# Feed-forward stage: rotating x in slices of 128 columns, with the 4-point levels on VectorE

## The chip, the cores and the metric

The kernel runs on one core of one Trainium2 chip. The metric is the device time of one execution in microseconds (us), lower is better. In the tables and rows PE is TensorE (PEld its weight load), DVE is VectorE, ACT is ScalarE, POOL is GpSimd and SP is SyncE.

## The reference

The input x is 128 batches of 32 tokens of 512 channels, 4096 rows in all. Three blocks are added to it in turn: cross attention over a context, a delta-rule attention with an MLP, and a feed-forward block. Only the last one is touched:

```python
def fwht(x):   # normalized Walsh-Hadamard transform of the last axis, n a power of 2
    h = 1
    while h < n:
        a, b = halves of each 2h columns
        x = stack([a + b, a - b]); h *= 2
    return x / sqrt(n)

def act_quant(x):  # per row
    scale = 127 / clip(max(abs(x)), EPS)
    return clip(round(x * scale), -128, 127) / scale

def h_bitlinear(x, w): return act_quant(fwht(x)) @ ternary(w).T

h = layernorm(x)                       # 512 wide
y = silu(h_bitlinear(h, w_gate)) * h_bitlinear(h, w_up)   # 2048 wide
x = x + h_bitlinear(y, w_down)         # 512 wide
```

So each row of h is rotated by a 512-point transform, and each row of y by a 2048-point one. Each is then rounded with a step that comes from the largest magnitude of its own row.

## The kernel before

Four phases follow one another: attention, delta rule, MLP, feed-forward (`ffn_phase`, line 1901). The MLP phase writes the normalised rows `xn`. The feed-forward phase works through 32 tiles of 128 rows (NT = 32). Five engine programs run side by side and hold a software pipeline: step k of each (`body(k, do)`) works on several tiles at once. Tile k is in its "main" part, tile k+1 in "one" (rotate and round x), tile k+2 in "two" (load and transpose x), tile k-1 in "mid" (butterflies of y on GpSimd), tile k-2 in "end" (round the rotated y, down projection) and tile k-3 in "sum". Steps -2 to 34 run, and an engine executes its instructions in the order written. Semaphores join the engines. PSUM banks are passed round in rings: `take` waits until a bank is full, `open` until it is free, `used` until it has been freed.

What each engine does in one step, in this order:

- TensorE: gates and ups of tile k (line 2008, 8 groups of four 512-column matmuls, through 4 banks), `rotate_x` of tile k+1 (line 1990), transposes of x of tile k+2 (1982), transposes of y (2017), of the first half of rounded z of tile k-2 (2034), `rotate_y` (2025) of the first half, transposes of the second half of z, `rotate_y` of the second half, transposes of rounded x (1999), down projection of tile k-2 (2042).
- ScalarE: waits for the factor of z (`q2`), then four times silu of a gate (2093) and scaling of a quarter of z (2096); the high part of xT (2101), four copies of yT (2105), scaling of the rotated x into `xs` (2109), then twice a copy of ziT (2114) and of zo (2118), and last the copy of xiT (2121).
- VectorE: largest magnitude of z (2217) with small operations for its factor, output sum (2211), four products y (2191) with the clipping of the first half of z (2186) in front of the last of them, the low part of xT (2179), the clipping of the second half of z (2186), then `round_x`: largest magnitude of the rotated x (2159) and five small operations (2161 to 2167). After it come `clip_x` (2174), which waits for `xs`, and `first_level`, four 512-column sums and differences (2202, 2203) in two pairs, each of which waits for ScalarE's zo.
- GpSimd: once `first_level` of tile k-1 is complete, six 1024-column sums and differences (2141 and 2142 in turn: zb, za, z), all with both operands in SBUF.

`rotate_x` takes the transposed x as a high and a low f16 part (`xT[:, 0]` and `xT[:, 1]`, n = 0, 1) and, for each of four 128-channel blocks c, multiplies it by 512 columns of the Hadamard matrix, all eight matmuls accumulating in one bank. That bank ("had", ring RX) is read by line 2159 on VectorE and by line 2109 on ScalarE, which frees it.

Of the kernel before, what the change touches and what calls it, by code (L numbers as in the profile page):

```python
# [7 lines left out]
P = 128  # L8
D = 512
DC = D // P  # L10
# [16 lines left out]
ALU = mybir.AluOpType  # L27
ACT = mybir.ActivationFunctionType
AXX = mybir.AxisListType.X


class Store:
# [6 lines left out]
    def sb(self, name, shape, dt=F32):  # L39
        return self.ctx.enter_context(self.nc.sbuf_tensor(self.tag + name, shape, dt))  # L40
# [4 lines left out]
    def sem(self, name):  # L45
        self.taken.append(self.ctx.enter_context(self.nc.semaphore(self.tag + name)))
        return self.taken[-1]
# [1853 lines left out]
def ffn_phase(nc, x2, xn, shared, out):  # L1901
# [5 lines left out]
    with ExitStack() as stack:  # L1907
# [8 lines left out]
        amax, step_, inv1, fac1 = (sb(n, [P, 1]) for n in ("amax", "step", "inv1", "fac1"))  # L1916
        gsc = sb("gsc", [P, 2])
        xs = sb("xs", [P, D])
        xq = sb("xq", [P, D], BF16)
        ident16 = sb("ident16", [P, P], BF16)  # L1920
        xiT = sb("xiT", [P, DC, P], BF16)
# [16 lines left out]
        y_ready, zo_ready, first, bf, am2, q2, zs_ready, clip2 = (  # L1938
            sem(n) for n in ("y_ready", "zo_ready", "first", "bf", "am2", "q2", "zs_ready", "clip2"))
        dsc_ready, summed = sem("dsc"), sem("summed")  # L1940

        def steps(eng, body):

# [30 lines left out]
        @block.tensor  # L1974
        def _(pe):
            pe.wait_ge(set_ready, 2)

            def transpose_x(i, r):
                p, full = RX.open(pe, r, "xT")
                pe.wait_ge(xn_ready, 16 * (i + 1))  # L1980
                for c in range(DC):
                    mm = pe.transpose(p[:, c * P:(c + 1) * P], xn_t[:, c * P:(c + 1) * P], ident[:])  # L1982
                mm.then_inc(full, 1)

            def rotate_x(i, r):
                RX.used(pe, r - 1, "xT")
                p, full = RX.open(pe, r, "had")
                for c in range(DC):
                    for n in range(2):
                        mm = pe.matmul(p[:], xT[:, n, c * P:(c + 1) * P], had[:, c, :],  # L1990
                                       start=(c + n == 0), stop=(c + n == DC))
                mm.then_inc(full, 1)

            def transpose_xi(i, r):
                p, full = RX.open(pe, r, "xiT")
                p = p[:].bitcast(BF16)
                pe.wait_ge(clip1, i + 1)
                for c in range(DC):
                    mm = pe.transpose(p[:, c * P:(c + 1) * P], xq[:, c * P:(c + 1) * P], ident16[:])
                mm.then_inc(full, 1)  # L2000

            def gates(i, r):
                RX.used(pe, r - 1, "xiT")
                for j in range(NB):
                    for n, w in (("g", w_g), ("u", w_u)):
                        p, full = RM.open(pe, i, f"{n}{j}")
                        for c in range(DC):
                            mm = pe.matmul(p[:], xiT[:, c, :], w[:, c, j * 512:(j + 1) * 512],  # L2008
                                           start=(c == 0), stop=(c == DC - 1))
                        mm.then_inc(full, 1)  # L2010

            def transpose_y(i):
                for j in range(NB):
                    p, full = RM.open(pe, i, f"yT{j}")
                    pe.wait_ge(y_ready, i * NB + j + 1)
                    for c in range(4 * j, 4 * j + 4):
                        mm = pe.transpose(p[:, c % 4 * P:(c % 4 + 1) * P], y[:, c * P:(c + 1) * P], ident[:])
                    mm.then_inc(full, 1)

            def rotate_y(i, js):  # L2020
                for j in js:
                    p, full = RM.open(pe, i, f"z{j}")
                    RM.used(pe, i, f"yT{j}")
                    for c in range(4):
                        mm = pe.matmul(p[:, c * P:(c + 1) * P], yT[:, 4 * j + c, :], had1, start=True, stop=True)  # L2025
                    mm.then_inc(full, 1)

            def transpose_zi(i, h):
                p, full = RQ.open(pe, i, f"zi{h}")
                p = p[:].bitcast(BF16)  # L2030
                pe.wait_ge(clip2, 2 * i + h + 1)
                for j in range(WC // 2):
                    c = WC // 2 * h + j
                    mm = pe.transpose(p[:, j * P:(j + 1) * P], zq[:, c * P:(c + 1) * P], ident16[:])
                mm.then_inc(full, 1)

            def down(i):
                p, full = RQ.open(pe, i, "down")
                for c in range(WC):
                    if c % (WC // 2) == 0:  # L2040
                        RQ.used(pe, i, f"zi{c // (WC // 2)}")
                    mm = pe.matmul(p[:], ziT[:, c, :], w_d[:, c, :], start=(c == 0), stop=(c == WC - 1))
                mm.then_inc(full, 1)
                RQ.skip(pe, i, "pad")

            def body(k, do):
                r = k + 2
                if do["main"]:
                    gates(k, r)
                if do["one"]:  # L2050
                    rotate_x(k + 1, r)
                else:
                    RX.skip(pe, r, "had")
                if do["two"]:
                    transpose_x(k + 2, r)
                else:
                    RX.skip(pe, r, "xT")
                if do["main"]:
                    transpose_y(k)
                if do["end"]:  # L2060
                    transpose_zi(k - 2, 0)
                if do["main"]:
                    rotate_y(k, (0, 1))
                if do["end"]:
                    transpose_zi(k - 2, 1)
                if do["main"]:
                    rotate_y(k, (2, 3))
                if do["one"]:
                    transpose_xi(k + 1, r)
                else:  # L2070
                    RX.skip(pe, r, "xiT")
                RX.skip(pe, r, "pad")
                if do["end"]:
                    down(k - 2)

            steps(pe, body)

        @block.scalar
        def _(act):
# [3 lines left out]
            def body(k, do):  # L2083
# [5 lines left out]
                for j in range(NB):  # L2089
                    if do["main"]:  # L2090
                        p, free = RM.take(act, k, f"g{j}")
                        act.wait_ge(y_ready, k * NB + max(j - 1, 0))
                        A.activation(sg[:, j % 2, :], p[:], ACT.Silu, scale=gsc[:, 0:1]).then_inc(free, 1)  # L2093
                    if do["end"]:
                        cols = slice(j * 512, (j + 1) * 512)
                        A.activation(zs[:, cols], z[:, cols], ACT.Identity, scale=fac2[:, 0:1], bias=offset[:, 0:1])\  # L2096
                            .then_inc(zs_ready, 1)
                if do["two"]:
                    p, _ = RX.take(act, r, "xT")
                    RX.take(act, r, "had")  # L2100
                    A.activation(xT[:, 0, :], p[:], ACT.Copy, scale=HS).then_inc(xT_hi, 1)  # L2101
# [3 lines left out]
                        A.copy(yT[:, 4 * j:4 * j + 4, :].rearrange("p c n -> p (c n)"), p[:]).then_inc(free, 1)  # L2105
                if do["one"]:
                    act.wait_ge(q1, 3 * (k + 2))
                    p, free = RX.take(act, r, "had")
                    A.activation(xs[:], p[:], ACT.Identity, scale=fac1[:, 0:1], bias=offset[:, 0:1]).then_inc(free, 1)
                for h in range(2):  # L2110
                    if do["end"]:
                        p, free = RQ.take(act, i, f"zi{h}")
# [36 lines left out]
        def _(dve):  # L2149
# [5 lines left out]

            def round_x(i, r):

                p, _ = RX.take(dve, r, "had")
                V.tensor_reduce(amax[:], p[:], AXX, ALU.max, apply_absolute_value=True).then_inc(am, 1)  # L2159
                dve.wait_ge(am, 3 * i + 1)  # L2160
                V.tensor_scalar(step_[:], amax[:], D ** -0.5 / HS, QEPS, ALU.mult, ALU.max).then_inc(am, 1)
                dve.wait_ge(am, 3 * i + 2)
                V.reciprocal(inv1[:], step_[:]).then_inc(am, 1)
                dve.wait_ge(am, 3 * i + 3)
                V.tensor_scalar(fac1[:], inv1[:], QMAX, D ** -0.5 / HS, ALU.mult, ALU.mult).then_inc(q1, 1)
                for n in range(2):
                    V.tensor_scalar(gsc[:, n:n + 1], step_[:], wscale[:, n:n + 1], 1.0 / QMAX, ALU.mult, ALU.mult)\
                        .then_inc(q1, 1)

            def clip_x(i, r):  # L2170
                RX.used(dve, r, "had")
                if not (isinstance(i, int) and i == 0):
                    RX.take(dve, r - 1, "xiT")
                V.tensor_scalar(xq[:], xs[:], MAGIC + QMAX, MAGIC, ALU.min, ALU.subtract).then_inc(clip1, 1)
# [164 lines left out]
```

## Time and profile before

| what | value |
|---|---|
| median of 3 runs | 3093.07 us (3091.05 to 3095.14) |
| profiled execution, own time | 3089.57 us |
| its span | 3087.7 us |
| PE busy over the span | 2757.9 us (89%) |
| DVE busy | 1990.8 us (64%) |
| ACT busy | 1436.7 us (47%) |
| POOL busy | 1009.8 us (33%) |

The span runs from the first to the last instruction that the profiler saw. The feed-forward phase begins about 2424 us into it and lasts to the end. Ends of matmuls are modelled, so a busy TensorE is not one at its peak; starts of successive groups are the better clock.

### The profile page before, as it was taken

What the parts mean: (1) busy time and instruction counts of PE and PEld (TensorE: products, weight loads), DVE (VectorE), ACT (ScalarE), POOL (GpSimd) and SP (SyncE); (2) the same over time, 40 slices, a digit from 0 to 9 for tenths busy, and PEclk for the clock granted to TensorE, in tenths of its full rate; (3) what the DMA queues carried; (4) which work ended last, traced back from release to release, by engine and by line L of the source; (5) the groups of instructions that cost most, each with busy time, mean ns of one, the idle gap of its engine ahead of it and who ended that gap; (6) DMA issues with size and microseconds to landing.
All of it is one profiled execution on the core that took longest, in us unless ns stands there. A gap on an engine that the chain in (4) does not pass through costs nothing. (4 is left out here: it accounts for less than half of the span.)

```text
span 3087.7 us, 66709 instructions
## 1 busy us (share of the span) xinstructions
PE 2757.9 (89%) x26968; PEld 1466.9 (48%) x26968; DVE 1990.8 (64%) x2991; ACT 1436.7 (47%) x2378; POOL 1009.8 (33%) x713
## 2 busy tenths in 40 slices
PE   6999999686888888888855999999999699999997
PEld 3444444252544444444433444444444366666664
DVE  3444444459989898898993544545543377777775
ACT  2222222375767758667632432222222256666664
POOL 0000000107538346274481000000000177777776
PEclk9999999888998989889866999999999899999998
DMA  6999888500000000000040032332120111111110
GB/s 241 336 334 332 312 284 310 176 15 1 2 29 2 29 13 19 29 2 29 16 155 21 22 111 94 101 104 96 66 71 28 66 38 41 41 41 41 41 37 31
DMA packets 126284, 290.20 MB, mean 94 GB/s; under 512 B 30480, under 2 KB 35216, under 8 KB 121968
## 3 DMA queue, kind: packets, MB, share of 16 engines
q1 hardware_dynamic: 122608, 261.85, 24.4%
q10 hardware_dynamic: 3456, 25.17, 2.4%
q8 instruction: 169, 2.77, 0.4%
q14 instruction: 51, 0.42, 0.0%
HBM read 244.96 MB, written 42.01 MB: 93 GB/s over the span
## 5 line engine op out<-in xcount | busy, mean ns | idle before, releaser
L2141 POOL TENSOR_TENSOR d_zb<-d_za 128x1024 f32<-128x1024 f32 x32 | 75.3, 2354 | 955.7 <-DVE d_za L2203 955.7
L899 PE MATMUL b_e<-b_hT,s_region 128*128 128x512 f16 x1152 | 283.3, 392 | 49.1 <-DVE s_region L1327 36.5
L1629 PE MATMUL c_r<-c_hT,c_g_pair 128*128 128x512 f16 x1056 | 244.4, 382 | 1.6 <-DVE c_hT L1805 1.6
L2008 PE MATMUL d_m<-s_region,d_xiT 128*128 128x512 bf16 x1024 | 238.4, 384 | 5.1 <-ACT d_xiT L2121 1.6
L1629 PE MATMUL c_r<-c_hT,c_u_pair 128*128 128x512 f16 x1056 | 242.3, 379 | 0.0
L1629 PE MATMUL c_d<-c_d_pair,c_aT 128*128 128x512 f16 x1056 | 242.1, 379 | 0.0
L1819 DVE SCALAR_TENSOR_TENSOR c_av<-c_r,c_sg 128x512 f32<-128x512 f32 x88 | 60.8, 691 | 271.7 <-PE c_r L1629 211.2
L1327 DVE SCALAR_TENSOR_TENSOR s_region<-b_e,b_cw,s_region 128x496 f32<-128x496 f32 (+2 forms) x288 | 203.0, 716 | 18.3 <-ACT s_region L1117 9.9
L851 POOL TENSOR_TENSOR b_tmp<-b_L,s_hn 128x496 f32<-128x496 f32 (+30 forms) x124 | 122.5, 988 | 260.9 <-ACT b_L L1100 251.5
L851 POOL TENSOR_TENSOR b_tmp<-b_L,b_U 128x496 f32<-128x496 f32 (+30 forms) x124 | 130.8, 1055 | 223.8 <-ACT b_L L1100 214.4
L899 PEld LDWEIGHTS b_e<-b_hT,s_region 128*128 128x128 f16 x1152 | 104.0, 100 | 190.0 <-DVE s_region L1327 44.2
L1729 ACT ACTIVATE c_sg<-c_r 128x512 f32<-128x512 f32 x88 | 52.5, 596 | 255.2 <-PE c_r L1629 255.1
L1629 PEld LDWEIGHTS c_r<-c_hT,c_g_pair 128*128 128x128 f16 x1056 | 103.8, 99 | 127.3 <-issue 2.8
L2008 PEld LDWEIGHTS d_m<-s_region,d_xiT 128*128 128x128 bf16 x1024 | 96.3, 99 | 141.6 <-DVEq L2194 16.3
L1629 PEld LDWEIGHTS c_r<-c_hT,c_u_pair 128*128 128x128 f16 x1056 | 103.3, 98 | 124.6
L268 POOL COPY a_kx<-a_kl 128x64 f32<-128x64 f32 x8 | 2.5, 313 | 485.3 <-PE a_ps L314 469.8
L1733 ACT CAST c_aT<-c_av 128x512 f16<-128x512 f32 x88 | 54.3, 617 | 229.5 <-DVE c_av L1819 229.5
L1629 PEld LDWEIGHTS c_d<-c_d_pair,c_aT 128*128 128x128 f16 x1056 | 103.3, 98 | 121.5 <-DVE c_aT L1824 0.2
L2093 ACT ACTIVATE d_sg<-d_m,d_gsc 128x512 f32<-128x512 f32 x128 | 87.2, 681 | 150.0 <-DVE d_fac L2223 140.6
L1377 DVE TENSOR_TENSOR b_U<-b_U,b_tmp 128x1488 f32<-128x1488 f32 (+30 forms) x124 | 145.4, 1172 | 4.3
L985 PE MATMUL b_r<-b_wo,b_xg 128*128 128x512 f32 x256 | 146.1, 688 | 0.0
L853 POOL TENSOR_TENSOR b_U<-b_U,b_tmp 128x496 f32<-128x496 f32 (+30 forms) x124 | 141.8, 1143 | 9.7
(255 smaller groups left out, 6029.7 us busy)
## 6 DMA issues: line engine op xcount, KB each, us to landing
a_cT<-in_ctxT SPq DMA_DIRECT2D x128, 512.0 KB, 9.7
a_cn<-in_ctx SPq DMA_DIRECT2D x128, 512.0 KB, 9.1
a_x_ln<-in_x SPq DMA_DIRECT2D x8, 1024.0 KB, 16.1
a_cw<-in_ctx SPq DMA_DIRECT2D x128, 64.0 KB, 9.5
a_x_res<-in_x SPq DMA_DIRECT2D x32, 256.0 KB, 11.4
x<-a_x_out SPq DMA_DIRECT2D x32, 256.0 KB, 11.3
b_xg<-x SPq DMA_DIRECT2D x8, 1024.0 KB, 5.5
om<-b_hT SPq DMA_DIRECT2D x32, 256.0 KB, 2.0
```

Source lines behind the costliest of these rows:

```text
L851: nc.gpsimd.tensor_tensor(tmp[:, QV, s + 1:S, :], lo, us, ALU.mult).then_inc(pool_prod, 1)
L853: nc.gpsimd.tensor_tensor(U[:, QV, s + 1:S, :], U[:, QV, s + 1:S, :], tmp[:, QV, s + 1:S, :], ALU.subtract).then_inc(pool_sub, 1)
L899: mm = pe.matmul(p[:], w_qkv[:, a, i, n, c * P:(c + 1) * P], hp[:, b, n, :], start=(n + a + b == 0), stop=(n == DC - 1 and a == 1))
L985: mm = pe.matmul(p[:], oT[:, c, t * P:(t + 1) * P], w_o[:, c, :], start=(c == 0), stop=(c == DC - 1))
L1327: ins = V.scalar_tensor_tensor(acc[:, :, j:S], src[:, :, 0:S - j], cw[:, i, c, TAPS - 1 - j:TAPS - j], acc[:, :, j:S], ALU.mult, ALU.add)
L1377: V.tensor_tensor(U[:, 0:QV, s + 1:S, :], U[:, 0:QV, s + 1:S, :], tmp[:, 0:QV, s + 1:S, :], ALU.subtract).then_inc(sub, 1)
L1629: mm = pe.matmul(out, x, y, start=start and i == 0, stop=stop and i == 2)
L1733: A.copy(aT[:, f % 2, 0, :], av[:]).then_inc(a_hi, 1)
L1819: V.scalar_tensor_tensor(av[:], p[:], AS / (WS * HS), sg[:, f % 2, :], ALU.mult, ALU.mult)\
L2008: mm = pe.matmul(p[:], xiT[:, c, :], w[:, c, j * 512:(j + 1) * 512], start=(c == 0), stop=(c == DC - 1))
L2093: A.activation(sg[:, j % 2, :], p[:], ACT.Silu, scale=gsc[:, 0:1]).then_inc(free, 1)
L2141: nc.gpsimd.tensor_tensor(o[:, :, 0, :], a[:, :, 0, :], a[:, :, 1, :], ALU.add).then_inc(bf, 1)
```

## The change

`rotate_x` multiplies each of the four 128-channel blocks by the 128-point Hadamard matrix alone and leaves the result in that block's own 128 columns of the bank. The eight matmuls keep their weights, and their columns go from 512 to 128. What is missing, a 4-point transform across the four slices, is done in two levels after it. ScalarE copies the odd slices (1 and 3) from PSUM to SBUF (`xo`, 256 columns). VectorE forms even + odd and even - odd from PSUM and `xo` into `xa`, two operations of 256 columns, and then frees the bank. From the two halves of `xa` it forms sum and difference into `xr`, again two operations of 256 columns, with both operands in SBUF. The largest magnitude is taken of `xr`, and ScalarE scales `xr` instead of the bank.

```diff
+        xo, xa, xr = sb("xo", [P, 2, P]), sb("xa", [P, 2, 2, P]), sb("xr", [P, 2, 2, P])
+        xo_ready, xl = sem("xo_ready"), sem("xl")
 rotate_x (TensorE):
-                        mm = pe.matmul(p[:], xT[:, n, c * P:(c + 1) * P], had[:, c, :],
-                                       start=(c + n == 0), stop=(c + n == DC))
+                        mm = pe.matmul(p[:, c * P:(c + 1) * P], xT[:, n, c * P:(c + 1) * P], had[:, 0, 0:P],
+                                       start=(n == 0), stop=(n == 1))
 body (ScalarE), between the scalings of z and the high part of xT:
+                if do["one"]:
+                    p, _ = RX.take(act, r, "had")
+                    A.copy(xo[:], p[:].rearrange("p (m two h) -> p m two h", two=2, h=P)[:, :, 1, :])\
+                        .then_inc(xo_ready, 1)
 body (ScalarE), scaling of x:
                 if do["one"]:
                     act.wait_ge(q1, 3 * (k + 2))
-                    p, free = RX.take(act, r, "had")
-                    A.activation(xs[:], p[:], ACT.Identity, scale=fac1[:, 0:1], bias=offset[:, 0:1]).then_inc(free, 1)
+                    A.activation(xs[:], xr[:].rearrange("p a b h -> p (a b h)"), ACT.Identity, scale=fac1[:, 0:1],
+                                 bias=offset[:, 0:1]).then_inc(xs_ready, 1)
 round_x (VectorE):
-                p, _ = RX.take(dve, r, "had")
-                V.tensor_reduce(amax[:], p[:], AXX, ALU.max, apply_absolute_value=True).then_inc(am, 1)
+                p, free = RX.take(dve, r, "had")
+                dve.wait_ge(xo_ready, i + 1)
+                even = p[:].rearrange("p (m two h) -> p m two h", two=2, h=P)[:, :, 0, :]
+                V.tensor_tensor(xa[:, :, 0, :], even, xo[:], ALU.add).then_inc(xl, 1)
+                V.tensor_tensor(xa[:, :, 1, :], even, xo[:], ALU.subtract).then_inc(xl, 1)
+                dve.wait_ge(xl, 4 * i + 2)
+                dve.sem_inc(free, 1)
+                V.tensor_tensor(xr[:, 0], xa[:, 0], xa[:, 1], ALU.add).then_inc(xl, 1)
+                V.tensor_tensor(xr[:, 1], xa[:, 0], xa[:, 1], ALU.subtract).then_inc(xl, 1)
+                dve.wait_ge(xl, 4 * i + 4)
+                V.tensor_reduce(amax[:], xr[:].rearrange("p a b h -> p (a b h)"), AXX, ALU.max, apply_absolute_value=True).then_inc(am, 1)
 clip_x (VectorE):
-                RX.used(dve, r, "had")
+                dve.wait_ge(xs_ready, i + 1)
```

## Rows read from the trace of the kernel before

**Rows 1.** Busy time by stretch: us, each engine's busy us (instructions), PEclk, DMA, GB/s
```profile
2500.00:2600.00 100.00, 99.45 (x657) 63.18 (x656) 76.41 (x122) 60.11 (x98) 75.79 (x32) 1.00 0.12 39
2900.00:3000.00 100.00, 99.61 (x655) 62.74 (x653) 76.01 (x122) 59.10 (x95) 75.57 (x32) 1.00 0.12 39
```
**Rows 2.** Timeline, one step, TensorE: start us, us, engine line op, tiles, [idle before]
```profile
2528.41 3.62 PE L2042 MATMUL d_q<-s_region,d_ziT 128*128 128x512 bf16 x16
2531.86 7.43 PE L2008 MATMUL d_m<-s_region,d_xiT 128*128 128x512 bf16 x32
2539.13 1.89 PE L1990 MATMUL d_x<-s_region,d_xT 128*128 128x512 f16 x8
2540.86 0.60 PE L1982 MATMUL d_x<-s_ident,d_xn 128*128 128x128 f32 x4
2543.04 0.61 PE L2034 MATMUL d_q<-d_ident,d_zq 128*128 128x128 bf16 x8
2543.49 2.00 PE L2025 MATMUL d_m<-s_region,d_yT 128*128 128x128 f32 x16
```
**Rows 3.** Timeline, the same step, VectorE and ScalarE, to the next first level
```profile
2530.34 0.68 DVE L2203 TENSOR_TENSOR d_za<-d_m,d_zo 128x512 f32<-128x512 f32 x1
2535.66 0.75 DVE L2191 SCALAR_TENSOR_TENSOR d_y<-d_m,d_gsc,d_sg 128x512 f32<-128x512 f32 x1
2539.02 2.05 DVE L2186 TENSOR_SCALAR d_zq<-d_zs 128x1024 bf16<-128x1024 f32 x1 [0.32 <-DVE d_y L2191]
2539.08 0.81 ACT L2096 ACTIVATE d_zs<-d_z,d_offset,d_fac 128x512 f32<-128x512 f32 x1
2540.99 0.74 DVE L2191 SCALAR_TENSOR_TENSOR d_y<-d_m,d_gsc,d_sg 128x512 f32<-128x512 f32 x1
2542.12 0.69 DVE L2179 SCALAR_TENSOR_TENSOR d_xT<-d_x,d_xT 128x512 f16<-128x512 f32 x1 [0.40 <-ACT d_xT L2101]
2542.73 1.12 DVE L2186 TENSOR_SCALAR d_zq<-d_zs 128x1024 bf16<-128x1024 f32 x1
2543.78 0.68 DVE L2159 TENSOR_REDUCE d_amax<-d_x 128x1 f32<-128x512 f32 x1
2545.31 0.78 ACT L2109 ACTIVATE d_xs<-d_x,d_offset,d_fac 128x512 f32<-128x512 f32 x1 [1.27 <-DVE d_gsc L2167]
2546.22 0.43 DVE L2174 TENSOR_SCALAR d_xq<-d_xs 128x512 bf16<-128x512 f32 x1 [0.95 <-ACT d_xs L2109]
2546.88 0.60 ACT L2118 COPY d_zo<-d_m 128x512 f32<-128x512 f32 x1
2547.67 0.69 DVE L2202 TENSOR_TENSOR d_za<-d_m,d_zo 128x512 f32<-128x512 f32 x1 [1.02 <-ACT d_zo L2118]
2549.79 0.68 DVE L2203 TENSOR_TENSOR d_za<-d_m,d_zo 128x512 f32<-128x512 f32 x1
```
**Rows 4.** Timeline, the same step, GpSimd: first and last three of its six
```profile
2531.10 2.36 POOL L2141 TENSOR_TENSOR d_zb<-d_za 128x1024 f32<-128x1024 f32 x1 [4.48 <-DVE d_za L2203]
2538.16 2.36 POOL L2142 TENSOR_TENSOR d_za<-d_zb 128x1024 f32<-128x1024 f32 x1
2540.75 2.55 POOL L2141 TENSOR_TENSOR d_z<-d_za 128x1024 f32<-128x1024 f32 x1 [0.24 <-POOL d_za L2142]
2543.26 2.80 POOL L2142 TENSOR_TENSOR d_z<-d_za 128x1024 f32<-128x1024 f32 x1
```
**Rows 5.** Timeline, delta phase: VectorE and GpSimd, both with two SBUF operands
```profile
1098.32 0.77 POOL L853 TENSOR_TENSOR b_U<-b_U,b_tmp 128x272 f32<-128x272 f32 x1
1099.17 1.73 POOL L851 TENSOR_TENSOR b_tmp<-b_L,b_U 128x256 f32<-128x256 f32 x1
1100.42 1.74 DVE L1377 TENSOR_TENSOR b_U<-b_U,b_tmp 128x1200 f32<-128x1200 f32 x1
```
**Rows 6.** Timeline, delta phase, GpSimd idle: VectorE sum and ScalarE copies near 256 columns
```profile
1406.91 0.35 ACT L1167 COPY s_xt<-b_e 128x256 f32<-128x256 f32 x1
1407.16 0.60 ACT L1168 COPY s_region<-b_e 128x256 f32<-128x256 f32 x1
...
1428.92 0.41 DVE L1377 TENSOR_TENSOR b_U<-b_U,b_tmp 128x240 f32<-128x240 f32 x1
```
**Rows 7.** Busy time by stretch at the phase's start (columns as in rows 1)
```profile
2468.00:2472.00 4.00, 2.18 (x19) 1.61 (x18) 3.79 (x4) 1.24 (x3) 1.76 (x1) 0.99 0.00 0
2472.00:2476.00 4.00, 4.00 (x13) 1.47 (x11) 3.62 (x7) 0.22 (x1) 3.11 (x2) 0.59 0.01 2
```

## The prediction

> **What bounds the kernel now.** The change lies wholly in the feed-forward phase, so I read that alone. The busy times by stretch come first: TensorE shows 99.5 busy in 100 us and VectorE 76 [rows 1], which invites the verdict that TensorE is the bound and that thinner matmuls help. The timeline of one step must confirm it. Steps repeat: `first_level` ends at 2530.34 + 0.68 = 2531.02 and next at 2549.79 + 0.68 = 2550.47 [rows 3], so a step takes 19.43 to 19.45 us. I call the first of these moments F, and give the rest as a distance from it.
>
> TensorE's order is full or nearly so. By starts, 16 down matmuls take 2531.86 - 2528.41 = 3.45 us, 216 ns each [rows 2]. The 32 gate matmuls take 2539.13 - 2531.86 = 7.27 us where 32 x 216 ns = 6.91, so TensorE stands about 0.36 us in each step, waiting in the middle of the gates for silu and y. It is not the sole bound, therefore.
>
> The other circle runs through VectorE, GpSimd and ScalarE. GpSimd starts its six operations at F + 0.07 [rows 4], and they set VectorE's pace. The fourth ends at 2538.16 + 2.36 = 2540.52, and the clip of the first half of z, issued at 2539.02, ends at 2541.07 [rows 3]: 0.55 us after GpSimd's operation. The fifth ends at 2543.30, and the second clip ends at 2543.85, again 0.55 after it. The sixth lasts 2.80 instead of the 2.36 of its kind, to 2546.06: it was held while the clip ran. So a clip and a GpSimd operation exclude each other, for whole instructions. The second clip ends at F + 12.82 because GpSimd's fifth ends at F + 12.27. From there a straight chain leads on: largest magnitude of x (2543.78), small operations, xs on ScalarE (2545.31), copies of ziT and zo (2546.88), first level (2547.67 to 2550.47) [rows 3], and that is the next F. Each member waits for the one before, as the idle times in the rows say. The clip, not TensorE, decides when the x rounding starts.
>
> **What is removed.** Eight matmuls of 512 columns take 2540.86 - 2539.13 = 1.73 us by starts. Eight transposes of 128 columns take 2543.49 - 2543.04 = 0.45 [rows 2]. That takes 1.28 us of TensorE's time in each step. Even at twice that length nothing below changes, as TensorE then has slack. What follows `rotate_x` is the transpose of x, its high part on ScalarE and the low part on VectorE, which idled 0.40 for it [rows 3]. It can now start when y is done, at 2541.73 and not at 2542.12. But the clip behind it still waits for GpSimd's fifth operation at F + 12.27. I cost the saving at nothing: behind that wait it disappears. If that cover were gone it would be worth at most the 0.40 us.
>
> **What ScalarE gets.** One copy of 256 columns from PSUM, at 0.6 us by the longer of two rows of that size, 0.35 by the shorter [rows 6]; I take the longer. It stands behind the last scaling of z, which ends at 2539.08 + 0.81 = F + 8.86. TensorE will have the thin rotation ready by 2539.13 + 0.45 = F + 8.55. So the copy lasts till about F + 9.5. Behind it are the high part of xT (0.6, till F + 10.1) and the yT copies. VectorE wants the high part at F + 10.7, so 0.6 us of cover is left, and a further 0.5 by the clip's wait. VectorE itself wants xo at F + 12.8. Cost of the copy and of the new wait: nothing, between 0 and 0.3 us a step if the cover should fail. Reading xs from SBUF instead of PSUM costs 0.81 against 0.78 [rows 3]: 0.03 us on the chain. The wait of clip_x for xs is the old one by another semaphore.
>
> **What VectorE gets.** Four operations of 256 columns, between the second clip and the largest magnitude, all on the chain. A 240-column sum takes 0.41 us [rows 6], a 512-column one 0.68, with 0.60 to 0.61 to the next start. That gives 0.27 us for 272 columns, 1 ns a column, so 256 columns take 0.43 alone and about 0.34 in a row. The bounds are 0.41 and 0.68 alone. The two xa operations have one operand in PSUM and one in SBUF, like the y products, which run at 0.74 to 0.75 beside a busy GpSimd [rows 3, 4]: they wait for nobody.
>
> The two xr operations have both operands in SBUF. The delta phase shows what becomes of such a pair beside GpSimd. A GpSimd sum of 256 columns takes 1.73 us there, where one of 272 took 0.77 just before. VectorE's 1200-column sum, issued at 1100.42, ends at 1102.16, and GpSimd's 256-column one had ended at 1099.17 + 1.73 = 1100.90 [rows 5]. The 1.26 us between are the 1200 columns alone. It stood until GpSimd's instruction was over, as the clips do.
>
> The Trainium skill speaks against this change on that point: its page "SBUF — State Buffer", section "Who interferes with whom", says that a VectorE instruction with two SBUF inputs contends with a GpSimd instruction that reads SBUF, and that the later one blocks in full. The trace agrees, by the 1.26 us above. Were only the faster modes of one-input instructions affected, the sum would be that of the first rival below.
>
> Now the sum. The clip ends at F + 12.82, and at that moment GpSimd's sixth operation, which had been waiting, takes its turn. The xa pair runs beside it, from 12.75 to 13.5, with 0.2 us for the wait and the release of the bank. The first xr is ready to go at about 13.7 and must wait for GpSimd's sixth to end, 2546.06 = F + 15.03 [rows 4]. It then needs 0.28, the second 0.34: F + 15.65. After 0.04 for the wait the largest magnitude starts at F + 15.69, against 2543.78 = F + 12.75 before. That is 2.94 us later, and with the 0.03 of xs 2.97 us a step. Nothing behind it can absorb that: GpSimd is idle, and ScalarE's and VectorE's orders are the old ones. TensorE, with 19.43 - 0.36 - 1.28 = 17.8 us of work in 22.4, will stand for rounded x, some 2.9 us in one piece, and for about 0.9 at the gates.
>
> How many steps: the 32 x tiles are rounded in steps -1 to 30. The full pattern, with the clips of z, runs in 2 to 30: 29 steps, 29 x 2.97 = 86 us. In steps -1 to 1 TensorE is late and gains some 2 us, and in step 1 the xr pair already meets GpSimd and loses 3. Net +1. Steps 31 on have no x. Sum +87. With the bounds of the 256-column operations, 0.41 to 0.68, the step gives 2.9 to 3.5 us, the sum 84 to 103. On the profiled execution: 3089.57 + 87 = 3176.6 us. The median of the runs shown, 3093.07, lies 3.5 above that execution, so for a median I add it: 3180.
>
> **The rivals.**
> *The xr pair isn't held.* Then the four operations cost their own time: 12.75 + 0.34 + 0.43 + 0.2 + 0.34 + 0.43 + 0.04 = 14.53 for the largest magnitude, 1.78 + 0.03 = 1.81 us a step, 29 x 1.81 = 52, less 2 at the start: 3143 as a median. For it: the VectorE rows in the delta phase show one clear overlap, not a proof for every layout. Against it: rows 5. 14 in 100.
> *Slower clock.* The granted clock was 0.59 in the 4 us after a stretch in which TensorE was busy for 2.18 of 4 [rows 7], that is, mostly at the 1.2 GHz level. The new pause of 2.9 us in each step could do so each time. Three us at that level lose 1.5 us of TensorE time in the down matmuls and the first gates, and the slack of 0.9 us plus what the y products leave covers it; that gives no loss. If the low level lasts 6 to 7 us, the down matmuls end 3.3 us later, the x transposes come at F + 11.1, the second clip is issued after GpSimd's sixth operation has begun and waits for that, and the step grows by another us: 3180 + 29 = 3209. 9 in 100. The Trainium skill ("TensorE: Matmul & The Clock Gate", Part 1) says that this clock has an idle level of 1.2 and a busy one of 2.4 GHz; rows 7 agree that it falls after pauses.
> *TensorE is the bound, and the time falls.* If the circle through VectorE had slack that the rows hide, every step would shrink by the matmuls' 1.28 us: 32 x 1.28 = 41, 3052. It would decide as soon as the additional VectorE work fitted into 18.15 us a step beside the rest. For it: 99.5 busy in 100 [rows 1]. Against it: ends of matmuls are modelled, there is the 0.36 us pause, and the chain from the clip to F has no gap. 5 in 100.
> *It balances.* The additions hide, the saving too: 3093. 3 in 100.
>
> **How the numbers follow.** Forecast 3180 with 66 in 100, and 3 for mishaps on the slow side. The range takes in the unheld pair with a few us (3136) and, on the upper side, the bound of 103 with the median's spread (3199); the forecast and the first rival together hold 80 in 100. A measurement of this kernel tells 0.2% (6 us) from no change. Faster 0.05, same 0.03, slower 0.92.
>
> **What would show it.** Right: line 1990 at some 0.5 us by starts; steps of 22.4 us between first levels; the first xr operation issued near F + 13.7 and lasting about 1.6 us, ending 0.3 after GpSimd's sixth; its second at 0.4; TensorE at about 80 in 100 with a pause ahead of the transposes of rounded x, released by the clip of x. Wrong: xr operations of 0.43 beside a running GpSimd (first rival); line 2179 waiting for ScalarE (the copy's cover fails); a granted clock well under 1.00 through the whole stretch with the second clip behind GpSimd's sixth (second rival); steps of 18 us (third).

## The result

The changed kernel takes 3180.02 us (median of 4 runs, 3176.92 to 3182.97) against 3094.11 of the kernel before in 4 runs: 1.0278 of it, with a 95% interval of 1.0260 to 1.0296. It is slower by 86 us. The profiled execution of the changed kernel took 3178.15 us with a span of 3176.3, 88.6 more than that of before in both.

Line numbers of after are higher: `rotate_x` is 1992, the copy of the odd slices 2102, the low part of xT 2194, the four level operations 2167, 2168, 2171 and 2172, the largest magnitude of x 2174, first level 2217 and 2218, clip of z 2201.

The same view as [rows 1], of after:

```profile
2500.00:2600.00 100.00, 87.20 (x577) 54.97 (x575) 77.45 (x124) 56.82 (x93) 68.60 (x29) 0.97 0.11 37
2900.00:3000.00 100.00, 86.60 (x557) 52.95 (x556) 77.54 (x125) 54.72 (x90) 66.18 (x28) 0.97 0.10 34
```

TensorE falls from 99.5 to 87 busy in 100 us, as a kernel does whose TensorE has been relieved, and yet everything takes longer: GpSimd, whose work is the same in each step, falls from 76 to 69. VectorE hardly changes in share, 76 to 77, because its new operations and the longer step nearly balance. None of these columns names the bound.

The timeline of one step of after, the counterpart of [rows 2 to 4], does (start us, us, engine, line, operation, tiles, idle time before):

```profile
2520.69 0.68 DVE L2218 TENSOR_TENSOR d_za<-d_m,d_zo 128x512 f32<-128x512 f32 x1
2521.45 2.36 POOL L2147 TENSOR_TENSOR d_zb<-d_za 128x1024 f32<-128x1024 f32 x1 [7.46 <-DVE d_za L2218]
...
2529.48 0.61 PE L1992 MATMUL d_x<-s_region,d_xT 128*128 128x128 f16 x8
2529.93 0.61 PE L1984 MATMUL d_x<-s_ident,d_xn 128*128 128x128 f32 x4
2530.15 0.37 ACT L2102 COPY d_xo<-d_x 128x256 f32<-128x256 f32 x1
2530.57 0.60 ACT L2107 ACTIVATE d_xT<-d_x 128x512 f16<-128x512 f32 x1
...
2532.43 0.69 DVE L2194 SCALAR_TENSOR_TENSOR d_xT<-d_x,d_xT 128x512 f16<-128x512 f32 x1 [0.35 <-DVE d_y L2206]
...
2533.04 1.15 DVE L2201 TENSOR_SCALAR d_zq<-d_zs 128x1024 bf16<-128x1024 f32 x1
2533.59 2.81 POOL L2148 TENSOR_TENSOR d_z<-d_za 128x1024 f32<-128x1024 f32 x1
2534.11 0.41 DVE L2167 TENSOR_TENSOR d_xa<-d_x,d_xo 128x256 f32<-128x256 f32 x1
2534.45 0.41 DVE L2168 TENSOR_TENSOR d_xa<-d_x,d_xo 128x256 f32<-128x256 f32 x1
2535.01 1.68 DVE L2171 TENSOR_TENSOR d_xr<-d_xa 128x256 f32<-128x256 f32 x1 [0.15 <-DVE d_xa L2168]
...
2536.61 0.41 DVE L2172 TENSOR_TENSOR d_xr<-d_xa 128x256 f32<-128x256 f32 x1
2537.06 0.69 DVE L2174 TENSOR_REDUCE d_amax<-d_xr 128x1 f32<-128x512 f32 x1
...
2540.12 0.59 PE L2001 MATMUL d_x<-d_ident,d_xq 128*128 128x128 bf16 x4 [2.62 <-DVE d_xq L2189]
...
2540.57 4.95 PE L2044 MATMUL d_q<-s_region,d_ziT 128*128 128x512 bf16 x16
...
2543.09 0.68 DVE L2218 TENSOR_TENSOR d_za<-d_m,d_zo 128x512 f32<-128x512 f32 x1
```

First levels end at 2521.37 and 2543.77: the step is 22.40 us where it was 19.44. With F = 2521.37, the clip of the second half of z ends at F + 12.82, as before to the hundredth. Behind it four rows stand where none stood. Three of them take 0.41 us. The fourth, line 2171, takes 1.68: GpSimd's sixth operation ends at 2533.59 + 2.81 = 2536.40, and line 2171 at 2536.69, 0.29 us later. The largest magnitude of x starts at F + 15.69; in the kernel before it was F + 12.75. TensorE's saving, and more, turns up as a pause of 2.62 us ahead of rounded x.

By line 2171, steps 3 to 30 start 22.33 to 22.44 us apart, all but the first of them within 0.04 us of one another. What costs time costs it in each step alike.

### The profile page after: what moved, and what is told of

It is laid out like the page before. It is cut to its first block and busy times, and to the rows that moved or that the text cites. A ratio compares the mean times of both kernels' runs of the same rounds, so it can differ in the third digit from the quotient of the medians.

```text
span 3176.3 us, 66955 instructions
## 1 busy us (share of the span) xinstructions
PE 2753.5 (87%) x26968; PEld 1463.7 (46%) x26968; DVE 2069.6 (65%) x3119; ACT 1452.6 (46%) x2410; POOL 1017.1 (32%) x713
## 5 line engine op out<-in xcount | busy, mean ns | idle before, releaser
L2044 PE MATMUL d_q<-s_region,d_ziT 128*128 128x512 bf16 x512 | 147.8, 454 | 1.1
```

## The experiments

All times below are medians, beside the kernel before on the same chip. The kernel before took 3093.91 us beside `levels_psum`, `narrow_only`, `wide_levels` and `copy_twice`, and 3092.01 beside `wide_fill` and the three of the last section.

### The same operations without two SBUF operands

`levels_psum` keeps four operations of 256 columns but pairs them otherwise. ScalarE copies the odd slices as they are and negated, so that one VectorE operation gives both the sum and the difference of a pair of slices. The lower pair's go to SBUF, the upper pair's into the used slices of the bank. Each operation of the second level then has one operand in PSUM and one in SBUF.

```diff
-                    A.copy(xo[:], odd slices).then_inc(xo_ready, 1)
+                    A.copy(xo[:, :, 0, :], odd).then_inc(xo_ready, 1)
+                    A.activation(xo[:, :, 1, :], odd, ACT.Copy, scale=-1.0).then_inc(xo_ready, 1)
...
-                V.tensor_tensor(xa[:, :, 0, :], even, xo[:], ALU.add).then_inc(xl, 1)
-                V.tensor_tensor(xa[:, :, 1, :], even, xo[:], ALU.subtract).then_inc(xl, 1)
+                V.tensor_tensor(xa[:], pv[:, 0, 0:1, :].to_broadcast([P, 2, P]), xo[:, 0], ALU.add).then_inc(xl, 1)
+                V.tensor_tensor(pv[:, :, 1, :], pv[:, 1, 0:1, :].to_broadcast([P, 2, P]), xo[:, 1], ALU.add).then_inc(xl, 1)
...
-                V.tensor_tensor(xr[:, 0], xa[:, 0], xa[:, 1], ALU.add).then_inc(xl, 1)
-                V.tensor_tensor(xr[:, 1], xa[:, 0], xa[:, 1], ALU.subtract).then_inc(xl, 1)
+                V.tensor_tensor(xr[:, 0], pv[:, :, 1, :], xa[:], ALU.add).then_inc(xl, 1)
+                V.tensor_tensor(xr[:, 1], xa[:], pv[:, :, 1, :], ALU.subtract).then_inc(xl, 1)
...
```

> The changed kernel with the same four 256-column operations on VectorE, but paired so that each has one operand in PSUM: ScalarE copies the odd slices as they are and negated, the first-level result of the upper pair of slices goes into the bank's used slices. My theory (the xr pair stands until GpSimd's sixth operation is over): the first xr operation takes 0.41 us and not 1.68, the step falls from 22.43 to about 21.2 us, the time from 3180 to about 3142. Rival (the 3 us a step are the number of VectorE operations and their waits, whatever the operands): still about 3180. The additional ScalarE copy of 0.4 us is to cost nothing by both.

Measured: 3141.62 us, 1.0153 of before (1.0136 to 1.0170). From step 4 on its steps are 21.14 to 21.18 us. Its timeline at the same place:

```profile
2526.75 2.81 POOL L2149 TENSOR_TENSOR d_z<-d_za 128x1024 f32<-128x1024 f32 x1
2527.26 0.41 DVE L2168 TENSOR_TENSOR d_xa<-d_x,d_xo 128x256 f32<-128x256 f32 x1
2527.59 0.41 DVE L2169 TENSOR_TENSOR d_x<-d_x,d_xo 128x256 f32<-128x256 f32 x1
2528.04 0.42 DVE L2171 TENSOR_TENSOR d_xr<-d_x,d_xa 128x256 f32<-128x256 f32 x1
2528.38 0.41 DVE L2172 TENSOR_TENSOR d_xr<-d_xa,d_x 128x256 f32<-128x256 f32 x1
2528.95 0.69 DVE L2175 TENSOR_REDUCE d_amax<-d_xr 128x1 f32<-128x512 f32 x1 [0.15 <-DVE d_xr L2172]
```

GpSimd's operation runs from 2526.75 to 2529.56, and all four VectorE operations run at full speed beside it. So line 2171 stood because its two operands lay in SBUF and GpSimd was running; the number of operations is the rest. The 2.99 us a step divide into 22.43 - 21.16 = 1.27 for the wait and 21.16 - 19.44 = 1.72 for the operations themselves. The second ScalarE copy costs nothing that can be seen.

### The saving alone

`narrow_only` is the kernel before with the narrow matmuls and nothing else. The transform across the slices is left out, so it computes something else.

```diff
-                        mm = pe.matmul(p[:], xT[:, n, c * P:(c + 1) * P], had[:, c, :], ...)
+                        mm = pe.matmul(p[:, c * P:(c + 1) * P], xT[:, n, c * P:(c + 1) * P], had[:, 0, 0:P], ...)
```

> The kernel before with the narrow rotation alone: eight matmuls of 128 columns, no levels across slices (the 4-point transform over the slices is left out; rounding and the rest run on what the bank holds). My theory (the circle through VectorE, GpSimd and ScalarE sets the step, so 1.28 us less on TensorE buy nothing): steps of 19.4 us, 3090 to 3094. Rival (TensorE, 99.5 busy in 100, is the bound): steps of 18.2 us, about 3053.

Measured: 3087.76 us, 0.9977 of before (0.9966 to 0.9988). That is a gain of 6 us, 2 us more than the expected range allows, and far from the 41 of the rival. Busy time by stretch (columns as in [rows 1]):

```profile
2500.00:2600.00 100.00, 94.06 (x648) 60.57 (x651) 75.72 (x123) 62.24 (x101) 75.97 (x32) 1.00 0.12 42
```

TensorE fell from 99.5 to 94 in 100, 1.05 us less in 19.44, and from step 4 on the steps are 19.42 to 19.46 us apart, as before. In the profiled execution the first x rounding starts 4.6 us later than in that of before (2437.17 against 2432.62), by phases that are the same in both, while its span is only 1.2 longer. So about 3.4 us are gained from there on, half in the first steps, where TensorE does set the time, and half in the last ones. The interval of the ratio begins at 3.7 us, so 3.4 from one pair of executions does not quite account for the 6; the rest stays open.

### The levels with the old rotation

`wide_levels` puts the 512-column matmuls back into the changed kernel.

```diff
-                        mm = pe.matmul(p[:, c * P:(c + 1) * P], xT[:, n, c * P:(c + 1) * P], had[:, 0, 0:P], ...)
+                        mm = pe.matmul(p[:], xT[:, n, c * P:(c + 1) * P], had[:, c, :], ...)
```

> The changed kernel with the old 512-column rotation in front of the new levels (the 4-point transform over the slices is done twice). My theory: the step stays at 22.4 us, since TensorE has some 4 us of slack in it; 3180 to 3184. Rival (the narrow matmuls already pay for part of the additions): the step grows by up to 1.3 us, up to 3218.

Measured: 3194.69 us, 1.0324 of before (1.0307 to 1.0342). This missed the expectation, 3180 to 3184. The steps are no longer equal. From start to start of line 2171 they are 21.2, 22.4, 23.5 and 24.8 us, but that line itself starts at another place in a step whose clip is late. By the largest magnitude of x behind it there are only two kinds: from step 3 on, 17 steps of 22.4 us and 11 of 23.5. One long step in its rows, first the busy time by stretch (PEclk is the third column from the right):

```profile
2517.00:2521.00 4.00, 1.45 (x10) 0.87 (x10) 1.89 (x8) 2.92 (x4) 0.00 (x0) 0.89 0.00 0
2521.00:2525.00 4.00, 4.00 (x14) 1.52 (x13) 3.24 (x5) 1.16 (x3) 1.65 (x1) 0.68 0.00 0
2525.00:2529.00 4.00, 4.00 (x20) 1.81 (x19) 3.33 (x8) 2.07 (x4) 3.92 (x3) 1.00 0.14 52
```

and then its timeline:

```profile
2519.60 0.38 PE L2001 MATMUL d_x<-d_ident,d_xq 128*128 128x128 bf16 x4 [2.20 <-DVE d_xq L2189]
...
2532.07 1.89 PE L1992 MATMUL d_x<-s_region,d_xT 128*128 128x512 f16 x8
...
2535.06 0.69 DVE L2194 SCALAR_TENSOR_TENSOR d_xT<-d_x,d_xT 128x512 f16<-128x512 f32 x1 [1.07 <-ACT d_xT L2107]
...
2535.53 2.36 POOL L2148 TENSOR_TENSOR d_z<-d_za 128x1024 f32<-128x1024 f32 x1
2535.67 2.76 DVE L2201 TENSOR_SCALAR d_zq<-d_zs 128x1024 bf16<-128x1024 f32 x1
```

TensorE stood 2.20 us for rounded x. The granted clock read 0.89 and then 0.68 of 2.4 GHz, so part of the down matmuls and gates ran at the 1.2 GHz level. VectorE had to wait 1.07 us for xT, and the second clip was issued at 2535.67, when GpSimd's sixth operation had begun at 2535.53. It ended after that one, at 2538.43, and not after the fifth. GpSimd then has nothing left to do, and line 2171 behind the clip takes 0.43 us:

```profile
2539.25 0.43 DVE L2171 TENSOR_TENSOR d_xr<-d_xa 128x256 f32<-128x256 f32 x1 [0.15 <-DVE d_xa L2168]
```

So the late clip costs 2.34 us (it ends 15.16 us after the first level and not 12.82) and spares the 1.26 of the held pair, which leaves the 1.1 us between the two kinds of step. Over the 9 us that begin 3 us behind the largest magnitude of x, the granted clock reads 0.81 in all 11 long steps, and 1.00 in 16 of the 17 others. This is the mechanism of the prediction's second rival. In the changed kernel the narrow rotation stands between it and the time.

### The pause filled

`wide_fill` tests that reading: twelve matmuls of constants in TensorE's pause.

```diff
                 if do["one"]:
+                    if do["end"]:
+                        fill, _ = RX.open(pe, r, "pad")
+                        for _ in range(12):
+                            pe.matmul(fill[:], had[:, 0, 0:P], had[:, 1, :], start=True, stop=True)
                     transpose_xi(k + 1, r)
```

> The kernel with the old 512-column rotation and the new levels (wide_levels), and in TensorE's pause ahead of the transposes of rounded x twelve further 512-column matmuls of constants into a bank that nobody reads (2.6 us of TensorE's time by 216 ns each). In wide_levels the steps alternate between 21.2, 22.4, 23.5 and 24.8 us, and the median is 3195. My theory (the granted clock falls after TensorE's pause, the late x transposes make the second clip miss GpSimd's fifth operation): with the pause filled the clock stays at 1.00, the steps are 22.4 us throughout and the time falls to 3180 to 3184 although TensorE has more to do. Rival (TensorE is short of time in itself with the wide rotation): the added work makes it slower, 3200 to 3230.

Measured: 3179.89 us, 1.0282 of before (1.0261 to 1.0304). TensorE does 2.6 us more in each step and the kernel is 15 us faster than `wide_levels` (13 by the two ratios). In the profiled executions 11.9 us of that lie between the first and the last x rounding, which is the 11 long steps. Busy time by stretch:

```profile
2500.00:2600.00 100.00, 97.75 (x605) 58.24 (x608) 77.92 (x124) 54.57 (x91) 65.29 (x27) 1.00 0.10 34
```

The clock is 1.00 where `wide_levels` has 0.95 in the same 100 us, and from step 4 on the steps are 22.40 to 22.45 us. With the clock held, the old rotation costs what the new one does: the 1.28 us saved on TensorE are worth nothing beside these levels. Without the filling they are worth the 15 us between `wide_levels` and the changed kernel. The changed kernel's own clock of 0.97 was harmless, as its equal steps show.

### ScalarE's copy twice

`copy_twice` makes the copy of the odd slices a second time, into a spare tile.

```diff
+                    act.wait_ge(xo_ready, 2 * (k + 1))
...
+                    A.copy(spare[:], odd slices of the bank).then_inc(xo_ready, 1)
...
-                dve.wait_ge(xo_ready, i + 1)
+                dve.wait_ge(xo_ready, 2 * i + 2)
```

> The changed kernel with ScalarE's copy of the odd slices made twice (the second into a spare tile, and VectorE waits for both). My theory (the copy lies in front of the high part of xT with more than 1 us of cover, 2531.17 against 2532.43 in the trace of after): 3180, steps of 22.4 us. Rival (ScalarE is part of the price): up to 0.3 us a step, up to 3190.

Measured: 3183.78 us, 1.0288 of before (1.0270 to 1.0305), 4 above the changed kernel with intervals that overlap. From step 4 on the steps are 22.40 to 22.44 us, the same. The profiled execution is 5.0 us longer than that of the changed kernel. The phase's first x rounding starts 3.4 us later (2437.82 against 2434.41), and the largest magnitude of step 1 comes 2.4 us later behind the one before it (20.43 us against 18.02). In that step, the first with GpSimd at work, the two xr operations meet GpSimd's fifth and sixth operation, and in the changed kernel its fourth and fifth. The same gap is 20.4 us in `wide_levels` and `wide_fill`, which copy once. In a full step the copy is free.

### The order on VectorE

If the second clip, tied to GpSimd's fifth operation, sets the step, then work that fits ahead of it is free, and what stands behind it is dear. Three kernels move work accordingly, with two moves at once whose shares they do not separate: the last y product goes ahead of the first clip (it was behind it), and something of the x rounding ahead of the second. In `narrow_y3` and `before_y3` that is the largest magnitude of x (`largest_x`, the `tensor_reduce` of `round_x`), in `psum_y3` the first two level operations.

```diff
                     if do["main"]:
                         gated(k, j)
-                    if do["end"] and j == 2:
+                    if do["end"] and j == 3:
                         clip_z(i, 0)
                 if do["two"]:
                     low_xT(k + 2, r)
+                if do["one"]:
+                    largest_x(k + 1, r)
                 if do["end"]:
                     clip_z(i, 1)
```

> The narrow rotation without the levels across slices (left out, as in narrow_only), and VectorE's order changed: the last y product before the first clip of z, and the largest magnitude of x ahead of the second clip. My theory (narrow_only gained little since the clip waits for GpSimd anyway; VectorE has about 1 us of idle time ahead of it): the low part of xT starts near F + 10.4, the largest magnitude is done before GpSimd's fifth operation ends, the clip still ends at F + 12.8, and the chain behind it is shorter by 0.6 us: steps of 18.8 us, 3069 to 3075. Rival (something other than the clip sets the step): 3088 as narrow_only.

Measured: 3066.77 us, 0.9910 of before (0.9893 to 0.9928), steps 6 to 29 of 18.78 to 18.80 us as expected, the time 2 us under the expected range. Like `narrow_only` it leaves the transform across the slices out. The timeline at the second clip:

```profile
2617.55 2.58 POOL L2141 TENSOR_TENSOR d_z<-d_za 128x1024 f32<-128x1024 f32 x1 [0.24 <-POOL d_za L2142]
2617.83 0.68 DVE L2181 SCALAR_TENSOR_TENSOR d_xT<-d_x,d_xT 128x512 f16<-128x512 f32 x1
2618.43 0.68 DVE L2158 TENSOR_REDUCE d_amax<-d_x 128x1 f32<-128x512 f32 x1
...
2619.03 1.65 DVE L2188 TENSOR_SCALAR d_zq<-d_zs 128x1024 bf16<-128x1024 f32 x1
2620.09 2.81 POOL L2142 TENSOR_TENSOR d_z<-d_za 128x1024 f32<-128x1024 f32 x1
2620.60 0.14 DVE L2163 TENSOR_SCALAR d_step<-d_amax 128x1 f32<-128x1 f32 x1
```

The clip still ends 0.55 us after GpSimd's fifth operation, at 2620.68, and the small operations follow at once: the 0.68 us of the largest magnitude has left the chain. Here the thin matmuls do buy something: with the wide ones and the same order, in the next kernel, the step is 19.07 us.

> The kernel before with the same change of VectorE's order alone, all of the computation in place. The x transposes come 1.28 us later than with the narrow rotation, the low part of xT starts at F + 11.1 and the largest magnitude ends near F + 12.3, when GpSimd's fifth operation ends too. My theory: the second clip is just too late, waits for the sixth, and ends near F + 15.1: steps of about 20 to 21 us, 3115 to 3145. If it is just in time: steps of 19.1 us, bound by TensorE, 3082 to 3086. Rival (the clips' wait for GpSimd is not what matters): 3094.

Measured: 3080.64 us, 0.9956 of before (0.9938 to 0.9973), with the whole of the computation in place. In the timeline the clip is just in time:

```profile
2602.72 2.82 POOL L2141 TENSOR_TENSOR d_z<-d_za 128x1024 f32<-128x1024 f32 x1 [0.24 <-POOL d_za L2142]
...
2604.88 0.68 DVE L2158 TENSOR_REDUCE d_amax<-d_x 128x1 f32<-128x512 f32 x1
2605.47 0.68 DVE L2188 TENSOR_SCALAR d_zq<-d_zs 128x1024 bf16<-128x1024 f32 x1
2605.50 2.87 POOL L2142 TENSOR_TENSOR d_z<-d_za 128x1024 f32<-128x1024 f32 x1
```

Steps 4 to 29 are 19.06 to 19.07 us, which is 19.43 less the 0.36 us pause. The 32 gate matmuls now take 6.91 us by starts (2594.37 to 2601.28), so the pause is gone: here TensorE is the bound, and the sum of its work is the step. This version beats both kernels, by 11 us and by 99. My first theory (too late by a hair) fell; the case named beside it held in its step, with the time 1 us under its range. The clip starts 0.02 to 0.04 us ahead of the sixth operation in every full step, and that is all the margin there is.

> levels_psum (3142 us, steps of 21.16 us) with VectorE's order changed: the last y product before the first clip of z, and the first pair of level operations ahead of the second clip. My theory: 0.75 us of the 1.73 us of additions move into VectorE's idle time ahead of the clip: steps of 20.4 us, 3117 to 3123. Rival (the pair is too late and the clip misses GpSimd's fifth operation): steps above 22 us, above 3165.

Measured: 3122.17 us, 1.0088 of before (1.0067 to 1.0109), steps 4 to 29 of 20.42 to 20.47 us. Of the 1.72 us of operations 0.73 went ahead of the clip. That is the best this study found for the narrow rotation with its levels, and it still loses to the kernel before.

## Why the prediction was right

The forecast was 3180 us, the measured median 3180.02. The span grew by 88.6 us where the sum said 87. That the last digits agree is luck: the four executions lie between 3176.92 and 3182.97, the profiled one took 1.6 us more than the 3176.6 worked out for it, and the median lies 1.9 us above it where I had added 3.5. What carries the forecast is the step, 2.99 us longer with 2.97 forecast.

*The bound.* Right. The circle through the second clip and GpSimd set the step, and TensorE with 99.5 in 100 was 0.36 us off being it: `narrow_only` shows it from the one side, `before_y3` with steps of 19.07 from the other.

*What is removed.* 1.28 us by starts were forecast. After shows 2529.93 - 2529.48 = 0.45 for the rotation against 1.73. Costed at nothing, and `wide_fill` (3179.89 with the wide rotation) confirms that for the steps. Three smaller things were off. I wrote that the low part of xT could start 0.40 us earlier; it starts at F + 11.06 against F + 11.10, since 0.35 us pass on VectorE between the y product and it even with xT long ready. The 0.40 us of idle time that [rows 3] put down to ScalarE were nearly all such passage. And "even at twice that length nothing below changes" left the clock out. No run has the rotation at twice its length; at nearly four times, the 1.73 us of `wide_levels`, 15 us are lost by the clock. And TensorE was to be at about 80 in 100, where 87 was measured: the pause is 2.62 us and not 2.9, and a part of the matmuls ran longer at the lower clock (below). None of the three touched the sum.

*ScalarE.* The copy was costed at nothing with 0.6 us of cover. It took 0.37, not 0.6, and the cover was 1.26 us (xT done at 2531.17, wanted at 2532.43). `copy_twice` found no cost in a step.

*VectorE.* 0.43 alone and 0.34 in a row were forecast; 0.41 and 0.34 measured. The release of the bank and its wait was put at 0.2 and was 0.15. The first xr was forecast to end 0.28 after GpSimd's sixth operation and ended 0.29 after it. The largest magnitude starts at F + 15.69, as forecast. Rows 5, two instructions from another phase, carried this term, and `levels_psum` shows that they were read rightly: 1.27 us of each step are the two SBUF operands. The forecast for the case without it, 3143, met the kernel without it, 3141.6.

*The rivals.* The unheld pair fell with line 2171's 1.68 us, TensorE as the bound with `narrow_only`. The slower clock existed, 0.97 in the stretches. Behind the pause of the step shown it read (columns as in [rows 1])

```profile
2539.00:2543.00 4.00, 2.88 (x10) 1.22 (x11) 2.23 (x4) 3.68 (x6) 0.00 (x0) 0.61 0.00 0
```

and the 16 down matmuls took 4.95 us where [rows 2] have 3.62. Steps with such a reading and steps without one are equally long, 22.4 us, so it cost the changed kernel nothing: the slack covered it, as the rival's first half said. That a longer delay would take the clip past GpSimd's sixth operation, for another 1.1 us a step, was right as a mechanism and was found one edit away. Its weight of 9 in 100 can't be judged from one outcome.

*The count.* 29 steps of 2.99 us make 86.7, and the span grew by 88.6. From the first tile's largest magnitude of x to the last tile's, the changed kernel takes 684.9 us and the kernel before 597.2, 87.7 more. Of these 4.2 fall in the three gaps up to step 2; less the 2.9 by which step 2's own levels delay it, about 1.2 is left for steps -1 to 1, near the forecast's +1. That is partly luck: where the xr pair meets GpSimd one operation later in step 1, as in `copy_twice`, it is 2.4 more. Behind the last one the changed kernel takes 1.7 us less (56.2 against 57.9). The sum had nothing there; `narrow_only` shows the same (56.0), so it is most likely TensorE's saving. Ahead of the first it takes 2.6 us more, its own levels included, which can't be told from the untouched phases: that first one starts between 2431.5 and 2439.2 in the ten profiled executions.

## What to carry to other kernels

An engine that is 99% busy in a stretch need not be what sets its time: follow a step from one fixed event to the next, and see which wait recurs with the same distance. Here an operation tied to another engine's instruction boundaries did it, so that work ahead of it was free and work behind it cost its full length; moving one reduction across it, with a y product moved to make room, gave 11 us where cutting the columns of eight matmuls to a quarter gave 6. Before putting an elementwise operation with both operands in SBUF on VectorE beside a busy GpSimd, look for a form with one operand in PSUM: the same four operations cost 1.27 us less a step.

## What the runs showed of the hardware that I had not expected

A pause of TensorE can cost more than its length, through another engine. In `wide_levels` a pause of 2.20 us brought the granted clock to 0.68 over 4 us, this made VectorE 1.07 us late, and the clip, issued 0.14 us after GpSimd's next instruction had begun, took 2.76 us instead of 1.15. Twelve useless matmuls in the pause took 15 us off the time. A pause of 2.62 us in the changed kernel brought the clock down as well and cost nothing, since nobody was late by it.

Where two VectorE instructions with both operands in SBUF stood in a row while GpSimd had more to do, GpSimd's next one got in between: in the first step with GpSimd at work the second xr operation took 2.57 us, the longest of its line. `copy_twice`, `wide_levels` and `wide_fill` show the same in that step, 2.56 us each. In the later steps GpSimd has finished its six by then, and it took 0.41. The two lines by themselves (ns shortest/median/longest over the 32 tiles):

```profile
L2171 DVE TENSOR_TENSOR d_xr<-d_xa x32: 426/1679/1691, 2434.4 to 3118.0; 128x256 f32<-128x256 f32 x32
L2172 DVE TENSOR_TENSOR d_xr<-d_xa x32: 410/411/2567, 2434.8 to 3119.6; 128x256 f32<-128x256 f32 x32
```

The shortest of line 2171, 426, is one to which GpSimd was no hindrance.
